# Where the three products of the second transform stand on TensorE in the spectrum of an image tokenizer

## The chip, the cores and the metric

The kernel runs on one core of one Trainium2 chip. The metric is device time in microseconds (us) of one execution; a time given for a kernel is the median of its runs.

## The reference

The reference takes 192 images (64 x 3 channels) of 224 x 224 values, forms the magnitude of their two-dimensional spectrum, crops it to 192 x 192 frequencies, sorts these by radius into 16 rings, projects each ring to a token, and then runs an attention layer, a second attention layer and a mixture of eight experts. Only the first line matters here; everything behind it is the same in both kernels.

```python
f = jnp.fft.fftshift(jnp.fft.fft2(images))
...
power = jnp.abs(f).astype(jnp.float32)
...
power_sorted = power.reshape(B, C, CROP * CROP)[:, :, idx]
```

## The kernel before

The first stage, the function `spectrum`, computes the magnitudes of the 97 x 97 frequencies that the symmetries leave. All data is float32. It works in units of two images (96 units), and two units make a group of four images (48 groups). Each of the five engines has a program of its own, written out by hand: a loop over units or groups, in which a step issues the work of several units at different lags. An engine takes its instructions strictly in this order, and counters (semaphores) tie the engines together. One unit u of group g passes through these places:

- SyncE loads the images of a group into `img`, a ring of four (L203).
- GpSimd adds the two halves of the group's images into `fold` (L255, the even part), and VectorE subtracts them (L367, the odd part). `fold` is a ring of two groups. They count `fold_done` and `odd_fold`.
- TensorE, first transform (`first_dft`, L288): eight products of 97 columns into the PSUM tile `ps1`, a ring of two units. Before the first of a group it waits for `fold_done` and `odd_fold` (L280, L281), and before each unit for `folded_done` at u - 1 (L282): the columns of unit u - 2 must have been folded, since `ps1` is used again. The last one counts `dft1_done`.
- ScalarE copies half of it to SBUF (`far`, L316), after `dft1_done`.
- VectorE folds the columns, one addition and one subtraction (`folded`, L360), and counts `folded_done`.
- TensorE, second transform (`second_dft`): one product of 388 columns (L297) and two of 194 columns (L300) into `ps2`, also a ring of two. It waits for `folded_done` of its unit and for `uv_done` at u - 1, that is, until the unit two before has been combined. The last one counts `dft2_done`.
- ScalarE copies the odd half to SBUF (`odd`, L321), after `dft2_done`; VectorE combines it with the even half (`uv`, L377) and counts `uv_done`; ScalarE squares (L328) and counts `sq_done`; GpSimd sums the squares of a group (`ss`, L262, two instructions); ScalarE takes the root into `power` (L334). SyncE then stores `power` to the table in HBM (L211).

Float32 products run as two passes each, so the trace has 16 first passes in a unit, then 2 of L297 and 4 of L300, and as many weight loads.

The order of each engine's step t is what the change and the prediction turn on:

- TensorE: first transform of unit t, then second transform of unit t - 2.
- ScalarE: `far` of t, `odd` of t - 2, square of t - 4, and in every second step (odd t) a root.
- VectorE: in every second step (even t) the odd part of the next group (L367), then columns of t, then combine of t - 2.
- GpSimd, by groups: even part of group g (L255), then the sum of group g - 3 (L262), which waits for the squares of that whole group.

Weights are loaded for every pass. In the first transform a piece of `fold` (112 columns) is the weight and the table of cosines and sines, `dft`, streams; in the second `dft` is the weight and `folded` streams.

After the stage, all engines wait until the table is stored, and GpSimd gathers the rings from it (L487).

Of the kernel before, what the change touches and what calls it, by code (L numbers as in the profile page):

```python
# [14 lines left out]
BATCH, CHANNELS, SIDE = 64, 3, 224  # L15
IMGS = BATCH * CHANNELS
HALF = SIDE // 2
CROP = 192
FREQ = CROP // 2 + 1
PAIR = 2 * FREQ  # L20
# [102 lines left out]
def at_least(eng, sem, n):  # L123

    if not (isinstance(n, int) and n <= 0):
        eng.wait_ge(sem, n)


def pipeline(eng, step, first, loops, end):


    for t in range(first):
        step(t, t)
    for start, stop, unroll in loops:
        with eng.Fori(start // unroll, stop // unroll) as body:
            for j in range(unroll):
                step(body * unroll + j, start + j)
        first = stop
    for t in range(first, end):
        step(t, t)  # L140
# [4 lines left out]
UNITS = IMGS // 2  # L145
# [5 lines left out]
UPG = G_IMGS // 2  # L151
# [3 lines left out]
Y_RING, FOLD_RING, A_RING, UV_RING, SS_RING = 4, 2, 4, 2, 2  # L155
BODY_G = 4
BODY_U = BODY_G * UPG
S2_LAG = 2
# [3 lines left out]
def spectrum(nc, ctx, sem, xh, table, dft_in, power, w_tok, wt, wt_in, load_constants):  # L162
# [6 lines left out]
    fold = sb("fold", [HALF, FOLD_RING, 2, G_IMGS * SIDE])  # L169
    dft = sb("dft", [HALF, PAIR])  # L170
    far = sb("far", [HALF, 2, 2, PAIR])
    folded = sb("folded", [HALF, A_RING, 2, 2, PAIR])
# [3 lines left out]
    ps1 = ctx.enter_context(nc.psum_tensor("ps1", [P, 2, 2, 512], F32))  # L176
    ps2 = ctx.enter_context(nc.psum_tensor("ps2", [P, 2, 2, 512], F32))
# [5 lines left out]
    dft1_done = sem("dft1_done")  # L183
    far_done = sem("far_done")
    folded_done = sem("folded_done")
    dft2_done = sem("dft2_done")
# [88 lines left out]
    def program_tensor(pe):  # L275
        pe.wait_ge(dft_in_s, 16)

        def first_dft(u, j):
            if j % UPG == 0:
                pe.wait_ge(fold_done, u // UPG + 1)  # L280
                pe.wait_ge(odd_fold, u // UPG + 1)  # L281
            at_least(pe, folded_done, u - 1)  # L282
            for i in range(2):
                for chunk in range(2):
                    for part in range(2):
                        x0 = ((j % UPG) * 2 + i) * SIDE + chunk * HALF
                        col = chunk * PAIR + part * FREQ
                        last = pe.matmul(ps1[0:HALF, j % 2, i, col:col + FREQ],  # L288
                                         fold[:, j // UPG % FOLD_RING, part, x0:x0 + HALF],
                                         dft[:, part * FREQ:(part + 1) * FREQ], start=True, stop=True)  # L290
            last.then_inc(dft1_done, 1)

        def second_dft(u, j):
            pe.wait_ge(folded_done, u + 1)
            at_least(pe, uv_done, u - 1)
            src = folded[:, j % A_RING]
            pe.matmul(ps2[0:FREQ, j % 2, 0, 0:2 * PAIR], dft[:, 0:FREQ], src[:, 0], start=True, stop=True)  # L297
            out = ps2[0:FREQ, j % 2, 1, 0:2 * PAIR].rearrange("p (i c) -> p i c", i=2)
            for part in range(2):
                last = pe.matmul(out[:, :, part * FREQ:(part + 1) * FREQ], dft[:, FREQ:PAIR],  # L300
                                 src[:, 1, :, (1 - part) * FREQ:(2 - part) * FREQ], start=True, stop=True)
            last.then_inc(dft2_done, 1)

        def step(t, j):
            if not isinstance(t, int) or t < UNITS:
                first_dft(t, j)
            if not isinstance(t, int) or t >= S2_LAG:
                second_dft(t - S2_LAG, j - S2_LAG)

        pipeline(pe, step, BODY_U, [(BODY_U, UNITS, BODY_U)], UNITS + S2_LAG)  # L310

    def program_scalar(act):
# [1376 lines left out]
```

## Time and profile before

| | us |
|---|---|
| runs of the kernel before | 925.77, 939.22, 938.95 |
| median | 938.95 |
| span of the profiled execution | 899.4 |
| median less span | 39.6 |
| spectrum stage in the profile, start to the last root | 312.9 |

The profile shows one execution; its own time is not listed, only the span from its first to its last instruction, and what lies around the span (launch and end) is not in the trace. In what follows "PE" is TensorE's stream of matmuls, "PEld" its weight loads, DVE VectorE, ACT ScalarE, POOL GpSimd. A bracket behind a row of the timeline is idle time of that engine just before the row, and what the profile takes for the end of it. The end of a matmul in the trace is modelled, so starts are the safer numbers.

### The profile page before, as it was taken

To read this page: it belongs to the slowest core of one execution; us is meant where nothing else is said; L and a number is where in the kernel's file an instruction comes from. 1 tells how busy PE (TensorE), PEld (TensorE's weight loads), DVE (VectorE), ACT (ScalarE), POOL (GpSimd) and SP (SyncE) were. 2 spreads that over 40 slices of the span, in tenths; PEclk is the share of its full clock that TensorE was granted. 3 is DMA by queue.
4 is the path that set the end of the run, shared out by engine and by line. 5 is a ranking of instruction groups with operands and counts; after the bars stand their busy time and mean duration, and the time that the engine had idled before them with its cause. 6 is when DMAs were issued, how large, how long until landed. Compare 5 with 4: busy or idle time off the path is not lost.

```text
span 899.4 us, 16681 instructions
## 1 busy us (share of the span) xinstructions
PE 737.3 (82%) x5723; PEld 628.5 (70%) x5724; DVE 543.7 (60%) x1003; ACT 429.6 (48%) x821; POOL 425.8 (47%) x363
## 2 busy tenths in 40 slices
PE   5999999999999502889988889968998659999920
PEld 4888888888888402878888886754666637999920
DVE  3899999999999404555555556986667431222224
ACT  1777777777777702444454443313122104555500
POOL 3577777777877407777777770021001161000044
PEclk9999999999999856899999999997669559999975
DMA  8844448854788177554555556000005531111112
GB/s 228 216 123 128 143 124 232 239 152 116 211 224 286 51 208 206 157 150 143 148 158 148 157 147 181 6 2 0 1 1 213 166 107 52 48 52 51 45 56 69
DMA packets 81353, 115.66 MB, mean 129 GB/s; under 512 B 10999, under 2 KB 61148, under 8 KB 80924
## 3 DMA queue, kind: packets, MB, share of 16 engines
q1 hardware_dynamic: 69918, 81.84, 32.0%
q0 software_dynamic: 11392, 33.24, 13.0%
q8 instruction: 28, 0.46, 0.2%
q14 instruction: 15, 0.12, 0.0%
HBM read 91.75 MB, written 23.30 MB: 128 GB/s over the span
## 4 chain that ended last, share of the span: by engine, by line
PE 44%; POOL 20%; DVE 18%; issue 9%; DMA 5%; ACT 2%; DVEq 0%; SPq 0%; POOLq 0%; ACTq 0%
POOL rows L487 15%; PE ps L288 10%; PE psum L1337 6%; DVE folded L360 4%; DVE fold L367 4%; PE ps L300 4%; PE ps L297 4%; PE psum L1324 4%; DVE uv L377 3%; PE psum L898 3%; DMA power_table<-power 3%; PE psum L1327 2%; POOL power L1270 2%; PE psum L919 2%; PE psum L907 2%
## 5 line engine op out<-in xcount | busy, mean ns | idle before, releaser
L546 PE MATMUL psum<-power,tT 128*128 128x192 f32 x864 | 157.9, 340 | 69.0 <-DVE tT L658 68.6
L546 PEld LDWEIGHTS psum<-power,tT 128*128 128x128 f32 x864 | 145.1, 197 | 79.2 <-issue 53.7
L288 PE MATMUL ps<-dft,fold 112*112 112x97 f32 x1536 | 170.9, 266 | 18.9 <-POOL fold L255 10.6
L288 PEld LDWEIGHTS ps<-dft,fold 112*112 112x112 f32 x1536 | 165.2, 181 | 27.6 <-DVE folded L360 15.3
L487 POOL DMA_INDIRECT rows<-power_table,rank_row x144 | 145.1, 1008 | 71.2 <-issue 43.3
L262 POOL TENSOR_TENSOR ss<-uv 97x388 f32<-97x388 f32 x96 | 119.4, 1266 | 77.9 <-ACT uv L328 77.9
L597 ACT ACTIVATE scaled<-rows,swaps 128x384 f32<-128x384 f32 x144 | 80.6, 607 | 127.6 <-DMA rows<-power_table,rank_row 127.5
L658 DVE SCALAR_TENSOR_TENSOR tT<-rows,swaps,scaled 128x384 f32<-128x384 f32 x144 | 82.7, 617 | 82.2 <-ACT scaled L597 80.8
L360 DVE TENSOR_TENSOR folded<-ps,far 112x388 f32<-112x388 f32 x192 | 98.6, 554 | 18.8 <-ACT far L316 18.8
L255 POOL TENSOR_TENSOR fold<-img 112x896 f32<-112x896 f32 x48 | 102.0, 2126 | 13.3 <-DMA img<-in_x 7.1
L377 DVE TENSOR_TENSOR uv<-ps,odd 97x388 f32<-97x388 f32 x192 | 98.6, 555 | 14.3 <-ACT odd L321 12.7
L367 DVE TENSOR_TENSOR fold<-img 112x896 f32<-112x896 f32 x48 | 79.4, 1653 | 9.0 <-DMA img<-in_x 9.0
L300 PEld LDWEIGHTS ps<-folded,dft 112*97 112x97 f32 x384 | 62.7, 163 | 31.5 <-issue 31.0
L328 ACT ACTIVATE uv<-uv 97x776 f32<-97x776 f32 x96 | 81.0, 845 | 0.0
L300 PE MATMUL ps<-folded,dft 112*97 112x194 f32 x384 | 79.1, 327 | 0.0
L297 PE MATMUL ps<-folded,dft 112*97 112x388 f32 x192 | 78.5, 491 | 0.4 <-DVE uv L377 0.4
L334 ACT ACTIVATE power<-ss 97x776 f32 (+1 forms) x48 | 75.7, 1577 | 0.4 <-POOL ss L262 0.4
L1270 POOL DMA_INDIRECT power<-expert_outputs,moe_slot x18 | 17.0, 945 | 123.6 <-DMA expert_outputs<-moe_y 118.5
L321 ACT ACTIVATE odd<-ps 97x388 f32<-97x388 f32 x96 | 47.1, 491 | 52.0 <-PE ps L300 52.0
L730 POOL TENSOR_SCALAR mv<-mv 128x3 f32<-128x3 f32 x6 | 1.5, 252 | 144.6 <-DVE mv L743 144.6
L316 ACT ACTIVATE far<-ps 112x388 f32<-112x388 f32 x96 | 49.0, 511 | 31.2 <-PE ps L288 31.2
L1363 ACT ACTIVATE z<-psum,moe_w_now 128x128 f32<-128x128 f32 x144 | 39.7, 375 | 33.3 <-PE psum L1327 33.1
(158 smaller groups left out, 923.0 us busy)
## 6 DMA issues: line engine op xcount, KB each, us to landing
img<-in_x SPq DMA_DIRECT2D x48, 784.0 KB, 5.2
power_table<-power SPq DMA_DIRECT2D x16, 576.0 KB
power<-in_w_tok SPq DMA_DIRECT2D x3, 1728.0 KB, 10.4
power_table<-power SPq DMA_DIRECT2D x1, 4656.0 KB
power<-in_w SPq DMA_DIRECT2D x8, 579.0 KB, 7.8
power<-in_w SPq DMA_DIRECT2D x4, 1152.0 KB, 10.7
rows<-power_table,rank_row POOLq DMA_INDIRECT x144, 3.1
expert_inputs<-zeros SPq DMA_DIRECT2D x1, 2304.0 KB, 11.0
```

The source lines that it names most:

```text
L255: pool.tensor_tensor(fold[:, j % FOLD_RING, 0], img[:, j % Y_RING, 0], img[:, j % Y_RING, 1], ALU.add).then_inc(fold_done, 1)
L262: last = pool.tensor_tensor(ss[:, j % SS_RING, s], uv[:, j % UV_RING, s, :, 0:FREQ], uv[:, j % UV_RING, 1 - s, :, FREQ:PAIR], ALU.add)
L288: last = pe.matmul(ps1[0:HALF, j % 2, i, col:col + FREQ], fold[:, j // UPG % FOLD_RING, part, x0:x0 + HALF], dft[:, part * FREQ:(part + 1) ...
L297: pe.matmul(ps2[0:FREQ, j % 2, 0, 0:2 * PAIR], dft[:, 0:FREQ], src[:, 0], start=True, stop=True)
L300: last = pe.matmul(out[:, :, part * FREQ:(part + 1) * FREQ], dft[:, FREQ:PAIR], src[:, 1, :, (1 - part) * FREQ:(2 - part) * FREQ], start=T ...
L328: act.activation(v, v, ACT.Square).then_inc(sq_done, 1)
L360: last = dve.tensor_tensor(folded[:, j % A_RING, part], near, far[:, j % 2], op)
L367: dve.tensor_tensor(fold[:, j % FOLD_RING, 1], img[:, j % Y_RING, 0], img[:, j % Y_RING, 1], ALU.subtract).then_inc(odd_fold, 1)
L377: last = dve.tensor_tensor(uv[:, j // UPG % UV_RING, part, i0:i0 + 2, :], even, odd[:, j % 2], op)
L487: pool.indirect_dma_start(out=rows[:, j % RING, half, :], out_offset=None, in_=table[0:RECORDS if j < PLAIN else ROWS, :], in_offset=bass. ...
L546: last = pe.matmul(ps[:, q % 2, 0:DIM], points[:, j % SWAPPED, c, s].rearrange("p h b -> p (h b)"), wt[:, c, s, chunk, :], start=(chunk == ...
L658: last = dve.scalar_tensor_tensor(out=points[:, j % SWAPPED].rearrange("p c s h b -> p (c s) h b")[:, :, half, :], in0=kept, scalar=swaps[ ...
```

## The change

On TensorE alone, a step no longer issues eight products of unit t and then three of unit t - 2. It first waits for all that either part needs, and then issues them mixed: two first products, the second transform's product of 388 columns, two first, one of 194, two first, the other of 194, two first. The products, their operands and their targets are the same, and so are the programs of the other engines. Two counters move with them: `dft2_done` is raised before the last two first products, and `dft1_done` at the very end of the step. The wait for `uv_done` moves from behind the eight first products to the head of the step.

```diff
-        def first_dft(u, j):
+        def first_ready(u, j):
             if j % UPG == 0:
                 pe.wait_ge(fold_done, u // UPG + 1)
                 pe.wait_ge(odd_fold, u // UPG + 1)
             at_least(pe, folded_done, u - 1)
...
-        def second_dft(u, j):
+        def second_ready(u):
             pe.wait_ge(folded_done, u + 1)
             at_least(pe, uv_done, u - 1)
...
         def step(t, j):
-            if not isinstance(t, int) or t < UNITS:
-                first_dft(t, j)
-            if not isinstance(t, int) or t >= S2_LAG:
-                second_dft(t - S2_LAG, j - S2_LAG)
+            dyn = not isinstance(t, int)
+            firsts, seconds = dyn or t < UNITS, dyn or t >= S2_LAG
+            if firsts:
+                first_ready(t, j)
+            if seconds:
+                second_ready(t - S2_LAG)
+            for n, (i, chunk, part) in enumerate((i, c, p) for i in range(2) for c in range(2) for p in range(2)):
+                if firsts:
+                    last = first_dft(j, i, chunk, part)
+                    if n == 7:
+                        last.then_inc(dft1_done, 1)
+                if seconds and n == 1:
+                    second_even(j - S2_LAG)
+                if seconds and n in (3, 5):
+                    last = second_odd(j - S2_LAG, n // 2 - 1)
+                    if n == 5:
+                        last.then_inc(dft2_done, 1)
```

`first_dft` now issues one product of the eight, `second_even` the product of 388 columns and `second_odd` one of the two of 194, with the operands that they had.

On TensorE, two steps in the loop of the stage before the change, an even one and the odd one behind it (`ps1` and `ps2` are the PSUM tiles of the first and the second transform; the names in brackets are the counters waited for):

```order
L126 REGISTER_ALU [waits odd_fold,fold_done]
L288 MATMUL ps1<-dft,fold 112x97 [waits folded_done]
L288 MATMUL ps1<-dft,fold 112x97 x7
L297 MATMUL ps2<-folded,dft 97x388 [waits uv_done,folded_done]
L300 MATMUL ps2<-folded,dft 97x2x97 x2
L288 MATMUL ps1<-dft,fold 112x97 [waits folded_done]
L288 MATMUL ps1<-dft,fold 112x97 x7
L297 MATMUL ps2<-folded,dft 97x388 [waits uv_done,folded_done]
L300 MATMUL ps2<-folded,dft 97x2x97 x2
```

And the even step and the head of the odd one at the same place after it:

```order
L126 REGISTER_ALU [waits odd_fold,fold_done]
L287 MATMUL ps1<-dft,fold 112x97 [waits uv_done,folded_done]
L287 MATMUL ps1<-dft,fold 112x97
L296 MATMUL ps2<-folded,dft 97x388
L287 MATMUL ps1<-dft,fold 112x97 x2
L301 MATMUL ps2<-folded,dft 97x2x97
L287 MATMUL ps1<-dft,fold 112x97 x2
L301 MATMUL ps2<-folded,dft 97x2x97
L287 MATMUL ps1<-dft,fold 112x97 x2
L287 MATMUL ps1<-dft,fold 112x97 [waits uv_done,folded_done]
L287 MATMUL ps1<-dft,fold 112x97
L296 MATMUL ps2<-folded,dft 97x388
```

The wait for `uv_done` has gone from the row of the 388-column product to the row that opens the step, and the step now ends with two products of the first transform, where it ended with two of the second.

The second place is the end of the stage on TensorE, from the last products of the loop's last step to the two steps that have no first transform left. Before:

```order
L288 MATMUL ps<-dft,fold 112x97 x7
L297 MATMUL ps<-folded,dft 97x388 [waits uv_done,folded_done]
L300 MATMUL ps<-folded,dft 97x2x97 x2
L135 REGISTER_ALU
L135 COMPARE_AND_BRANCH
L297 MATMUL ps<-folded,dft 97x388 [waits uv_done,folded_done]
L300 MATMUL ps<-folded,dft 97x2x97 x2
```

And after:

```order
L287 MATMUL ps<-dft,fold 112x97 x2
L301 MATMUL ps<-folded,dft 97x2x97
L287 MATMUL ps<-dft,fold 112x97 x2
L135 REGISTER_ALU
L135 COMPARE_AND_BRANCH
L296 MATMUL ps<-folded,dft 97x388 [waits uv_done,folded_done]
L301 MATMUL ps<-folded,dft 97x2x97 x2
```

The last products of the first transform now stand directly ahead of the next step's second transform, where three longer products stood between. The program of ScalarE, which waits for both counters, is the same row for row: `far` of unit t, then `odd` of unit t - 2, then the square of unit t - 4.

## Rows read from the trace of the kernel before

**Rows 1.** The page: the span of the profiled execution.

```profile
span 899.4 us, 16681 instructions
```

**Rows 2.** Windows of the stage: busy us (instructions) by engine, granted clock, DMA.

```profile
200.00:300.00 100.00, 97.00 (x728) 82.88 (x726) 90.13 (x147) 78.00 (x117) 75.46 (x50) 1.00 0.69 205
```

**Rows 3.** Waits until 310 us: engine, line, releaser, us in total, times, longest.

```profile
POOL ss L262 <- ACT uv L328: 77.9, 48, 6.2
...
PEld ps L300 <- issue: 31.0, 192, 0.2
...
PE ps L288 <- DVE folded L360: 8.3, 22, 0.4
...
PE ps L297 <- DVE uv L377: 0.4, 1, 0.4
```

**Rows 4.** Timeline: start, us, engine, line, tiles; TensorE and the way to its wait.

```profile
144.23 1.81 PE L288 MATMUL ps<-dft,fold 112*112 112x97 f32 x16 [0.41 <-DVE folded L360]
...
147.19 1.72 PE L288 MATMUL ps<-dft,fold 112*112 112x97 f32 x16
...
150.06 1.72 PE L288 MATMUL ps<-dft,fold 112*112 112x97 f32 x16
150.26 0.49 ACT L321 ACTIVATE odd<-ps 97x388 f32<-97x388 f32 x1 [0.82 <-PE ps L300]
...
150.65 0.84 ACT L328 ACTIVATE uv<-uv 97x776 f32<-97x776 f32 x1
...
151.57 2.56 POOL L262 TENSOR_TENSOR ss<-uv 97x388 f32<-97x388 f32 x2 [1.79 <-ACT uv L328]
151.62 0.82 PE L297 MATMUL ps<-folded,dft 112*97 112x388 f32 x2
...
152.27 0.82 PE L300 MATMUL ps<-folded,dft 112*97 112x194 f32 x4
...
152.94 1.72 PE L288 MATMUL ps<-dft,fold 112*112 112x97 f32 x16
...
154.09 2.09 POOL L255 TENSOR_TENSOR fold<-img 112x896 f32<-112x896 f32 x1
...
156.31 1.81 PE L288 MATMUL ps<-dft,fold 112*112 112x97 f32 x16 [0.34 <-DVE folded L360]
...
168.56 0.63 PE L288 MATMUL ps<-dft,fold 112*112 112x97 f32 x4 [0.43 <-DVE folded L360]
```

**Rows 5.** Timeline of the same steps: weight loads, ScalarE and VectorE between them.

```profile
151.74 1.65 DVE L367 TENSOR_TENSOR fold<-img 112x896 f32<-112x896 f32 x1
...
152.77 0.53 ACT L316 ACTIVATE far<-ps 112x388 f32<-112x388 f32 x1
152.77 1.72 PEld L288 LDWEIGHTS ps<-dft,fold 112*112 112x112 f32 x16
...
153.20 0.48 ACT L321 ACTIVATE odd<-ps 97x388 f32<-97x388 f32 x1
153.34 1.03 DVE L360 TENSOR_TENSOR folded<-ps,far 112x388 f32<-112x388 f32 x2
...
154.28 1.02 DVE L377 TENSOR_TENSOR uv<-ps,odd 97x388 f32<-97x388 f32 x2
...
154.69 0.49 ACT L316 ACTIVATE far<-ps 112x388 f32<-112x388 f32 x1 [0.27 <-PE ps L288]
...
155.22 1.03 DVE L360 TENSOR_TENSOR folded<-ps,far 112x388 f32<-112x388 f32 x2
```

**Rows 6.** Timeline at the end of the stage, its last two steps.

```profile
300.58 0.49 ACT L316 ACTIVATE far<-ps 112x388 f32<-112x388 f32 x1 [0.29 <-PE ps L288]
...
301.70 0.81 PE L297 MATMUL ps<-folded,dft 112*97 112x388 f32 x2
...
302.42 1.03 DVE L377 TENSOR_TENSOR uv<-ps,odd 97x388 f32<-97x388 f32 x2 [0.28 <-ACT odd L321]
...
303.60 0.86 PE L297 MATMUL ps<-folded,dft 112*97 112x388 f32 x2 [0.43 <-DVE uv L377]
```

More of the change, by code:

```diff
@@ L282, in first_dft @@
             at_least(pe, folded_done, u - 1)
[L283 to L290, printed above, removed]
@@ L291, in first_dft @@
-            last.then_inc(dft1_done, 1)
-        def second_dft(u, j):
+        def first_dft(j, i, chunk, part):
+            x0 = ((j % UPG) * 2 + i) * SIDE + chunk * HALF
+            col = chunk * PAIR + part * FREQ
+            return pe.matmul(ps1[0:HALF, j % 2, i, col:col + FREQ],
+                             fold[:, j // UPG % FOLD_RING, part, x0:x0 + HALF],
+                             dft[:, part * FREQ:(part + 1) * FREQ], start=True, stop=True)
+        def second_ready(u):
             pe.wait_ge(folded_done, u + 1)
@@ L295, in second_dft, with second_even, second_odd @@
             at_least(pe, uv_done, u - 1)
-            src = folded[:, j % A_RING]
-            pe.matmul(ps2[0:FREQ, j % 2, 0, 0:2 * PAIR], dft[:, 0:FREQ], src[:, 0], start=True, stop=True)
+        def second_even(j):
+            return pe.matmul(ps2[0:FREQ, j % 2, 0, 0:2 * PAIR], dft[:, 0:FREQ], folded[:, j % A_RING, 0],
+                             start=True, stop=True)
+        def second_odd(j, part):
             out = ps2[0:FREQ, j % 2, 1, 0:2 * PAIR].rearrange("p (i c) -> p i c", i=2)
-            for part in range(2):
-                last = pe.matmul(out[:, :, part * FREQ:(part + 1) * FREQ], dft[:, FREQ:PAIR],
-                                 src[:, 1, :, (1 - part) * FREQ:(2 - part) * FREQ], start=True, stop=True)
@@ L302, in second_dft @@
-            last.then_inc(dft2_done, 1)
+            return pe.matmul(out[:, :, part * FREQ:(part + 1) * FREQ], dft[:, FREQ:PAIR],
+                             folded[:, j % A_RING, 1, :, (1 - part) * FREQ:(2 - part) * FREQ], start=True, stop=True)
         def step(t, j):
-            if not isinstance(t, int) or t < UNITS:
-                first_dft(t, j)
-            if not isinstance(t, int) or t >= S2_LAG:
-                second_dft(t - S2_LAG, j - S2_LAG)
+            dyn = not isinstance(t, int)
```

## The prediction

> **What bounds the kernel now.** I read the page first, then the windows of the stage, the waits, and a timeline of some steps, row by row. The span is 899.4 us [rows 1]; the stage that the change touches lies in its first third. In it TensorE is busy 97 us of 100, VectorE 90, ScalarE 78 and GpSimd 75, at full granted clock (1.00, the level of 2.4 GHz) [rows 2]. That looks like a stage bound by TensorE, but 97% of a busy engine isn't yet a bound: it also waits, 22 times, for 8.3 us together [rows 3]. So the timeline has to say what a round of the pipeline costs, and what closes it.
>
> A step of TensorE that starts without a wait takes 2.87 us (147.19 to 150.06), one behind a wait 2.96 (144.23 to 147.19) [rows 4]. Four steps of 2.87 would be 11.48. The rows that wait stand at 144.23, 156.31 and 168.56 [rows 4]: four steps apart, two groups, 12.08 and 12.25 us, mean 12.17. A round of four steps thus has some 0.6 us that isn't TensorE's own work, half a microsecond of waiting and a slower first step.
>
> Who is waited for? The profile names the folding of the columns (L360). The counter in the code says otherwise. The unit that starts at 156.31 is number 48 (counting the 16-pass rows from the start); it asks for `folded_done` 47, that is, units 0 to 46, and the columns of unit 46 end at 153.34 + 1.03 = 154.37 [rows 5]. It also opens a group, and so asks for the even part of that group, which GpSimd makes from 154.09 to 156.18 [rows 4]; 0.13 later TensorE starts. The columns row that ends at 156.25 (155.22 + 1.03) belongs to unit 47, which this step doesn't need [rows 5].
>
> So follow GpSimd back [rows 4]. Its even part (154.09) is queued behind a sum (151.57, 2.56 us); that sum waited for the squares of its group, which is also the longest wait of the whole stage, 77.9 us in 48 times [rows 3]; the square starts at 150.65, the copy `odd` ahead of it at 150.26, and that one waited for TensorE: the end of the step whose successor starts at 150.06. The way from there to 156.31 is 0.20 + 0.39 + 0.92 + 2.52 + 2.22 = 6.25 us. With the two steps before it, 144.23 to 150.06 = 5.83, it makes 12.08: the round. The bound of this stage is a ring of TensorE (two steps), ScalarE (`odd`, square) and GpSimd (sum, even part), and TensorE's throughput lies 5% under it.
>
> **The change part by part.** Nothing is added or removed in work. Three things move, and each touches the ring.
>
> First, `dft1_done` now comes at the end of a step, and ScalarE asks for it (`far` of t) before it looks at `dft2_done` (`odd` of t - 2). Before, `far` was copied while TensorE was still at the second transform, and `odd` started 0.20 us behind the step. Now both counters are late together: `far` follows the last first product. Today `far` starts at 154.69, 0.03 after the end of its 16 passes (152.94 + 1.72) [rows 4, 5]. A pass is 1.56 / 16 = 0.098 us (150.06 to 151.62) and the last of a run ends 0.16 after its successor could start (1.72 - 1.56), so `far` will start about 0.20 after the step's end, where `odd` stands now, and `odd` behind it: 153.20 - 152.77 = 0.43 later [rows 5]. That `dft2_done` itself is raised earlier brings nothing, as `odd` stands behind `far` in ScalarE's queue. Price: 0.43 us in each round. Bounds: 0 (if `far` were copied beside something) and 0.53 (its full duration); I take the row's 0.43. The two others that ask for `dft1_done`, the even and the odd part of the group after next, stay covered: the first products of the step that ends at 150.06 would be through some 0.2 later, and these parts start at 154.09 and 151.74 [rows 4, 5].
>
> Second, the order of the passes. A first pass streams 97 columns; by the 388-column product, 0.65 for two passes (151.62 to 152.27), that is 0.65 / 2 / 4 = 0.081 us of streaming [rows 4], yet it takes 0.098, because a weight load stands before each. Behind a long product the first such load has already been done. Before, a step has one run of first passes behind long ones; after, three, two of which begin inside the step. Each saves at most 0.098 - 0.081 = 0.017, so about 0.03 in a step and 0.06 in the two steps of the ring. Bounds: no gain, and 16 x 0.017 = 0.27 in a step if all loads were hidden. Against the second end stands that weight loads of L300 sat idle for 31.0 us in 192 cases for nothing but their issue [rows 3]: two per unit, 0.16 each, while a long product streamed, so loads aren't drawn further ahead than one.
>
> Third, the wait for `uv_done` stands at the step's head. Before, it came behind eight products and cost 0.4 us once [rows 3]. Now a step t needs the combine of t - 4. Odd steps: `far` at 0.20 behind the step's end, columns 0.53 later (154.69 to 155.22), the combine ends 1.96 after the columns' start (153.34 to 154.28 + 1.02) [rows 5], so 2.69 in all, against 2.84 for the next step's end. Weight loads lead their matmuls by 0.17 (152.77 against 152.94) [rows 4, 5], and from GpSimd's end to TensorE's start it was 0.13; 2.69 + 0.13 + 0.17 - 2.84 = 0.15, so this costs from 0 to 0.15 in an odd step. Even steps: VectorE has the odd part of a group before the columns (151.74 to 153.34 = 1.60), so 2.69 + 1.60 + 1.96 = 6.25 after the end of the odd step; the GpSimd way will take 6.25 + 0.43 = 6.68. Covered by 0.43, while that cover holds. Queued behind the waiting product are the eleven of its own step; who waits for those is `far`, then `odd`. I take 0 for this edit, and 0.15 for its upper end. TensorE would idle near 0.9 us in 12.5 where it idles 0.5 in 12.2; with its clock granted at 1.00 beside that, I count nothing for the clock.
>
> The sum for a round: 0.43 - 0.06 = 0.37 us. One wait to a round, 22 waits [rows 3] are 88 of the 96 steps: 22 x 0.37 = 8.1. The other eight, at the start, save 8 x 0.03 = 0.2. At the end, the last `far` starts at 300.58 and the last second transform, at 303.60, waited for a combine that ends at 302.42 + 1.03 = 303.45, 0.15 before [rows 6]. In the new order that `far` comes 0.20 behind the last step (301.70 + 0.20 = 301.90), its columns at 302.43, the combine behind them ends 1.96 later at 304.39, and TensorE goes on 0.15 after that, at 304.54: 0.9 later. Sum 8.1 - 0.2 + 0.9 = 8.8 us. Everything behind the stage waits for its store, so the span goes from 899.4 to 908.2. The profiled execution's own time isn't given; I put the same 8.8 on the median: 938.95 + 8.8 = 947.8. The three runs spread from 925.77 to 939.22, more than the effect; a change of less than 2% (18.8 us) can hardly be told from none here.
>
> **The rivals.** *VectorE closes the ring after all* (slower). If the profile's naming is right, and TensorE is released by the columns of unit 47, then the way is `odd` at 150.26, combine, odd part, columns, combine, columns [rows 4, 5]. With `far` ahead, VectorE does the columns of unit 45 before that combine, which then ends at 2.69 instead of 151.74 - 150.06 = 1.68 behind the step: 1.01 - 0.06 = 0.95 a round, 22 x 0.95 + 0.7 = 21.6, 960.6 us. It decides once VectorE's way is over 0.43 longer than I have it. For it: VectorE is busy 90 of 100, and the profile's naming; against it: the counter's value, and GpSimd's even part ending 0.13 before the start.
>
> *All loads hidden* (not slower). If loads are drawn under the long products that now stand between the first ones, a step falls by up to 0.27 and a round by 0.54, less 0.43: 22 x -0.11 = -2.4, with -8 x 0.27 = -2.2 at the start and 0.9 at the end -3.7, so 935.2 us. Against it stand the 31.0 us in which loads sat idle beside long products [rows 3]. For it speaks the Trainium skill, page "TensorE: Matmul & The Clock Gate", section "Back-to-back issue gap": matmuls and weight loads are pipelined through a window of 64 instructions; the trace doesn't agree with so deep a look ahead, by those 31.0 us.
>
> *Throughput was the bound* (not slower): the waits are slack elsewhere, and only the 0.03 of a step counts, 96 x 0.03 = 2.9: 936.1. Against it: the 22 waits, each two groups apart.
>
> **How the numbers follow.** Forecast 0.72 (947.8; own range 934.6, which is 925.77 + 8.8, to 953.6, with 0.15 in odd steps and 0.53 for `far`: 22 x 0.25 = 5.5 more, and 0.3, the higher run above the median). VectorE 0.13, loads 0.08, throughput 0.07. The range 934 to 957 holds the forecast, both not-slower cases, and of the VectorE case only what comes when its cover is gone in part. Slower by over 2% is nearly all of that case, 0.12; faster by over 2% needs a low run on top of a gain, 0.02; within 2% is 0.86.
>
> **What would show it.** Right: rounds of 12.5 us; `far` 0.2 behind each step's end, `odd` 0.4 behind `far`; TensorE's idle time before L287 about doubled; the last root ending near 322, against 312.9. Wrong: rounds of 12.1 or less, or of 13 with the combine as what ends the wait.

## The result, and the profile after

The changed kernel takes 944.36 us (median of 22 runs, 931.25 to 955.30) beside 939.09 us (median of 22 runs, 919.38 to 949.31) for the kernel before. Some executions of either kernel, disturbed ones, take some 1.5% longer; the comparison leaves them out, which the two medians don't. By it the ratio is 1.0106, with a 95% interval of 1.0085 to 1.0128, that is 8.0 to 12.0 us of 939, the middle 10.0. The forecast was 8.8 us, and within 2%.

The profile after is one execution of 954.42 us:

```profile
span 952.6 us, 16705 instructions
```

Its span lies 53.2 us above that of [rows 1], which isn't what the change costs. The last root of the stage ends at 320.66 + 1.51 = 322.17 us, where it was 312.87; the stage is 9.3 us longer. The other 43.9 us lie behind it, in code that is the same, where the granted clock differs. Two windows of that part, before and after:

```profile
450.00:550.00 100.00, 88.38 (x539) 81.88 (x538) 55.86 (x87) 46.57 (x87) 67.90 (x69) 1.00 0.51 143
```

```profile
450.00:550.00 100.00, 76.86 (x407) 72.62 (x407) 46.45 (x74) 39.22 (x75) 61.42 (x60) 0.85 0.42 119
```

The third number from the end is the granted clock: 1.00 in that execution of before, 0.85 here, a mean over stretches at either level. In the ten profiles of this study the part behind the stage, the same code in all, took from 587 us (mean clock 0.900 over the span) to 630 us (0.875). So spans can't be compared across these profiles, but the stage can: its clock is 1.00 in all of the loop. I compare by the round, four steps of TensorE, as a mean of 20 rounds from the first pass of step 12 to that of step 92: 46.96 to 290.12 before, 12.158 us; 47.24 to 298.91 after, 12.584. The round is 0.43 us longer; the forecast was 0.37.

The window of the stage, to be read beside [rows 2], busy us (instructions) by engine in the order PE, PEld, DVE, ACT, POOL, then clock and DMA:

```profile
200.00:300.00 100.00, 93.55 (x700) 81.53 (x699) 78.99 (x144) 74.34 (x113) 73.22 (x49) 1.00 0.69 202
```

TensorE's share falls from 97 to 94 with nothing else rising: everyone waits more, so a chain of waits has grown and no engine has. VectorE falls by eleven points, far more than the stage slows; that is told at the end.

The waits until 322 us, beside [rows 3]:

```profile
ACT far L329 <- PE ps L287: 93.0, 74, 12.4
POOL ss L262 <- ACT uv L341: 86.4, 48, 5.2
...
PE ps L287 <- POOL fold L255: 27.9, 23, 11.1
```

TensorE's wait now bears GpSimd's name, which in [rows 3] was VectorE's: 27.9 - 11.1 (the wait for the first image) = 16.8 us in 22 times, where it was 8.3 in 22. And `far` waits for TensorE 74 times, where it was 51, since its counter comes at the step's end.

The timeline of the round that answers to [rows 4]: start, us, engine, line, operation, tiles, and in brackets the idle time before:

```profile
147.94 0.60 PE L287 MATMUL ps<-dft,fold 112*112 112x97 f32 x4 [0.76 <-POOL fold L255]
...
153.31 1.07 PE L287 MATMUL ps<-dft,fold 112*112 112x97 f32 x8
...
153.88 0.49 ACT L329 ACTIVATE far<-ps 112x388 f32<-112x388 f32 x1 [1.23 <-PE ps L287]
...
154.27 0.49 ACT L334 ACTIVATE odd<-ps 97x388 f32<-97x388 f32 x1
...
154.65 0.85 ACT L341 ACTIVATE uv<-uv 97x776 f32<-97x776 f32 x1
...
155.58 2.55 POOL L262 TENSOR_TENSOR ss<-uv 97x388 f32<-97x388 f32 x2 [2.04 <-ACT uv L341]
...
156.29 1.10 DVE L380 TENSOR_TENSOR fold<-img 112x896 f32<-112x896 f32 x1
...
158.09 2.08 POOL L255 TENSOR_TENSOR fold<-img 112x896 f32<-112x896 f32 x1
...
158.34 1.02 DVE L390 TENSOR_TENSOR uv<-ps,odd 97x388 f32<-97x388 f32 x2
...
160.24 1.03 DVE L373 TENSOR_TENSOR folded<-ps,far 112x388 f32<-112x388 f32 x2 [0.88 <-ACT far L329]
...
160.51 0.63 PE L287 MATMUL ps<-dft,fold 112*112 112x97 f32 x4 [0.83 <-POOL fold L255]
```

The row at 153.31 holds the last two products of one step (four passes) and the first two of the next, so the step ends about 4 x 0.098 = 0.39 later, at 153.70. (The row takes 1.07, where eight such passes in a row without a wait take 0.93: the next step, too, starts a little late. That start isn't in the ring.) From there: `far` 0.18 behind, `odd` 0.39 behind `far`, square 0.38, sum 0.93, even part 2.51, next step 2.42: 6.81 us, where [rows 4] had 6.25. The two steps ahead of it take 153.70 - 147.94 = 5.76, where they took 5.83. Three terms can be seen: `far` in front of `odd`, 0.39; the two steps, -0.07; and TensorE starts 160.51 - 160.17 = 0.34 behind the end of the even part, where that was 0.13. Over all groups the median of that distance is 0.24. The last term was in no sum of mine.

The same three terms as means over the 20 rounds, with a step's end taken as the start of its last pass and 0.098 us, or 0.165 where that pass has 194 columns: `odd` starts 0.59 behind the step's end, where it was 0.24, so 0.35; the two steps take 5.75, where they took 5.83, so -0.08; TensorE starts 0.28 behind the even part, where it was 0.13, so 0.15. Together they are 0.42 of the 0.43.

The row at 160.24 also settles whether TensorE asks for the columns that the profile named: they are those of the unit just before, and they end at 161.27, when the step that opens at 160.51 has long been running.

### The profile page after: what moved, and what is told of

The parts are those of the page before. It is cut to its first block, busy times and chain, and to the rows that moved or that the text cites. A ratio compares the mean times of both kernels' runs of the same rounds, so it can differ in the third digit from the quotient of the medians.

```text
span 952.6 us, 16705 instructions
## 1 busy us (share of the span) xinstructions
PE 752.9 (79%) x5723; PEld 649.3 (68%) x5724; DVE 515.3 (54%) x1003; ACT 426.2 (45%) x821; POOL 427.0 (45%) x363
## 4 chain that ended last, share of the span: by engine, by line
PE 52%; issue 16%; POOL 15%; DVE 8%; DMA 3%; another core or an unknown queue 2%; ACT 2%; POOLq 1%; ACTq 0%; DVEq 0%; SPq 0%
PE psum L559 16%; POOL fold L255 8%; PE psum L1350 5%; PE ps L287 5%; POOL ss L262 4%; PE psum L1337 3%; PE psum L911 3%; DMA power_table<-power 2%; PE psum L1340 2%; PE ps L301 2%; PE ps L296 2%; PE psum L542 2%; POOL power L1283 2%; PE psum L932 2%
## 5 line engine op out<-in xcount | busy, mean ns | idle before, releaser
L559 PE MATMUL psum<-power,tT 128*128 128x192 f32 x864 | 171.2, 358 | 91.2 <-DVE tT L671 58.7
L287 PEld LDWEIGHTS ps<-dft,fold 112*112 112x112 f32 x1536 | 197.9, 179 | 63.6 <-issue 47.4
L559 PEld LDWEIGHTS psum<-power,tT 128*128 128x128 f32 x864 | 160.0, 212 | 97.2 <-issue 78.1
L287 PE MATMUL ps<-dft,fold 112*112 112x97 f32 x1536 | 203.6, 262 | 28.7 <-POOL fold L255 27.9
L262 POOL TENSOR_TENSOR ss<-uv 97x388 f32<-97x388 f32 x96 | 119.5, 1267 | 86.4 <-ACT uv L341 86.4
L610 ACT ACTIVATE scaled<-rows,swaps 128x384 f32<-128x384 f32 x144 | 77.8, 604 | 62.9 <-DMA rows<-power_table,rank_row 48.5
L301 PE MATMUL ps<-folded,dft 112*97 112x194 f32 x384 | 94.9, 328 | 0.0
L296 PE MATMUL ps<-folded,dft 112*97 112x388 f32 x192 | 78.6, 491 | 1.3 <-DVE uv L390 1.3
L380 DVE TENSOR_TENSOR fold<-img 112x896 f32<-112x896 f32 x48 | 54.4, 1134 | 9.9 <-DMA img<-in_x 9.9
L1350 PE MATMUL psum<-power,z 128*128 x288 | 53.0, 335 | 0.0
L301 PEld LDWEIGHTS ps<-folded,dft 112*97 112x97 f32 x384 | 48.7, 166 | 0.7 <-issue 0.6
```

The source lines that it names most:

```text
L262: last = pool.tensor_tensor(ss[:, j % SS_RING, s], uv[:, j % UV_RING, s, :, 0:FREQ], uv[:, j % UV_RING, 1 - s, :, FREQ:PAIR], ALU.add)
L287: return pe.matmul(ps1[0:HALF, j % 2, i, col:col + FREQ], fold[:, j // UPG % FOLD_RING, part, x0:x0 + HALF], dft[:, part * FREQ:(part + 1) ...
L296: return pe.matmul(ps2[0:FREQ, j % 2, 0, 0:2 * PAIR], dft[:, 0:FREQ], folded[:, j % A_RING, 0], start=True, stop=True)
L301: return pe.matmul(out[:, :, part * FREQ:(part + 1) * FREQ], dft[:, FREQ:PAIR], folded[:, j % A_RING, 1, :, (1 - part) * FREQ:(2 - part) * ...
L559: last = pe.matmul(ps[:, q % 2, 0:DIM], points[:, j % SWAPPED, c, s].rearrange("p h b -> p (h b)"), wt[:, c, s, chunk, :], start=(chunk == ...
L1350: last = pe.matmul(psum[:, 6 + j % 2, 0:DIM], hT[:, j % 2, m * P:(m + 1) * P], w2[:, bass.ds(e, 1), m, :].rearrange("p a n -> p (a n)"), s ...
```

## The experiments

Each kernel changes one thing and is read by the round. In brackets behind a round stand the starts of steps 12 and 92, 20 rounds apart. The counters are those of the code: `dft1_done` after the first transform, `dft2_done` after the second, `uv_done` after the combine.

**The copy `far` out of the ring's way.** Edit on the changed kernel:

```diff
-                if seconds and n in (3, 5):
-                    last = second_odd(j - S2_LAG, n // 2 - 1)
-                    if n == 5:
+                if seconds and n in (3, 7):
+                    last = second_odd(j - S2_LAG, n // 4)
+                    if n == 7:
```

> The changed kernel, but the second product of 194 columns stands behind all eight first products, so that dft1_done comes before the step's end and dft2_done at it, as in the kernel before; the interleaving and the waits at the step's head stay. A round is four steps of TensorE, the mean from unit 12 to unit 92: 12.16 us before, 12.58 after. Theory (the copy far, queued ahead of odd on ScalarE, lengthens the ring by 0.39): far is copied 0.1 to 0.2 earlier than the step's end, odd starts 0.2 to 0.3 behind it, and the round falls to 12.2 to 12.3. Rival (mixing itself, weight changes or PSUM traffic, costs): the round stays at 12.5 to 12.6. Rival (the waits at the head alone): it stays at 12.5 or more.

Measured: round 12.274 us (47.17 to 292.65). The timeline:

```profile
145.40 0.60 PE L287 MATMUL ps<-dft,fold 112*112 112x97 f32 x4 [0.67 <-POOL fold L255]
...
151.02 0.49 ACT L329 ACTIVATE far<-ps 112x388 f32<-112x388 f32 x1 [1.23 <-PE ps L287]
151.16 0.54 PE L287 MATMUL ps<-dft,fold 112*112 112x97 f32 x4
...
151.41 0.49 ACT L334 ACTIVATE odd<-ps 97x388 f32<-97x388 f32 x1
...
157.64 0.53 PE L287 MATMUL ps<-dft,fold 112*112 112x97 f32 x3 [0.63 <-POOL fold L255]
```

`far` starts 0.14 before the next step (151.16) instead of 0.18 behind, and `odd` 0.25 behind it instead of 0.57. That takes 0.31 of the 0.43 away with the products still mixed. So 0.31 of the loss hangs on which counter is raised last, and none of that on the mixing.

**No mixing, but the same counter last.** Edit on the changed kernel, in the place of its loop over n:

```diff
+            if seconds:
+                second_even(j - S2_LAG)
+                second_odd(j - S2_LAG, 0)
+                second_odd(j - S2_LAG, 1).then_inc(dft2_done, 1)
+            if firsts:
+                for i, chunk, part in ((i, c, p) for i in range(2) for c in range(2) for p in range(2)):
+                    last = first_dft(j, i, chunk, part)
+                last.then_inc(dft1_done, 1)
```

> No mixing at all: the three products of the second transform stand ahead of the eight of the first, with the same waits at the step's head as in the changed kernel. dft1_done comes at the step's end, dft2_done 1.6 us before. Theory (far ahead of odd): the round is 12.5 to 12.7, like the changed kernel's, though nothing is mixed; odd starts 0.39 behind far and far 0.2 behind the step's end. Rival (mixing costs): the round is 12.2 or less.

Measured: round 12.631 us (48.69 to 301.30). The second transform now opens a step (L296 rows):

```profile
149.75 0.86 PE L296 MATMUL ps<-folded,dft 112*97 112x388 f32 x2 [0.72 <-POOL fold L255]
...
152.67 0.82 PE L296 MATMUL ps<-folded,dft 112*97 112x388 f32 x2
...
155.61 0.86 PE L296 MATMUL ps<-folded,dft 112*97 112x388 f32 x2
155.74 0.49 ACT L326 ACTIVATE far<-ps 112x388 f32<-112x388 f32 x1 [1.26 <-PE ps L287]
156.13 0.49 ACT L331 ACTIVATE odd<-ps 97x388 f32<-97x388 f32 x1
...
162.37 0.89 PE L296 MATMUL ps<-folded,dft 112*97 112x388 f32 x2 [0.81 <-POOL fold L255]
```

The row at 155.74 is `far`, right behind the step's end; `odd` follows 0.39 later, though its own products stand at the head of the step that began at 152.67. The loss is all there without any mixing, and 0.05 more, since the mixing's small gain is gone. The rival that mixing itself costs falls with these two runs.

**The wait at the step's head.** Edit on the changed kernel:

```diff
             if seconds:
-                second_ready(t - S2_LAG)
...
                 if seconds and n == 1:
+                    at_least(pe, uv_done, t - S2_LAG - 1)
                     second_even(j - S2_LAG)
```

The two steps without a first transform keep their wait for `folded_done`.

> The changed kernel with the wait for uv_done taken from the step's head to the product of 388 columns, where it stood before, and the doubled wait for folded_done (it asks for the same count) left out; the order of products stays. If the row of waits at the head costs what it seems to (TensorE starts 0.24 to 0.37 behind GpSimd's even part, where it was 0.13), that gap falls to about 0.13 and the round by 0.1 to 0.2, to 12.4 to 12.5, and the second group of a round no longer waits for the combine. If the head's waits cost nothing, the round stays at 12.58.

Measured: round 12.440 us (47.40 to 296.21), 0.14 less. The rows behind a sum:

```profile
157.09 2.08 POOL L255 TENSOR_TENSOR fold<-img 112x896 f32<-112x896 f32 x1
...
159.31 0.63 PE L287 MATMUL ps<-dft,fold 112*112 112x97 f32 x4 [0.63 <-POOL fold L255]
```

TensorE starts 159.31 - 159.17 = 0.14 behind the even part, close to the 0.13 before the change. So more waits queued behind the one that ends last delay the start, though they had long been met: the combine of the step at 160.51 in the changed kernel ended at 158.34 + 1.02 = 159.36, 1.15 before. Which of the two waits taken out does it isn't told apart.

**Both edits together.** The two diffs above at once.

> Both single edits at once on the changed kernel: the second product of 194 columns behind all eight first ones, and the wait for uv_done at the product of 388 columns. Alone they took the round from 12.58 us to 12.27 and to 12.44. If they are two separate terms of one ring, their gains add: 12.58 - 0.31 - 0.14 = 12.13, under the 12.16 of the kernel before by about what the mixing saves TensorE; GpSimd's even part is again 0.13 ahead of the step. If they are one and the same delay seen twice, the round stays near 12.27.

Measured: round 12.135 us (46.65 to 289.35), where 12.13 was expected, so the terms add: 0.31 + 0.14 = 0.45. That is 0.02 under the kernel before, with the products mixed. The rows behind a sum:

```profile
151.79 1.09 DVE L377 TENSOR_TENSOR fold<-img 112x896 f32<-112x896 f32 x1
...
153.58 2.09 POOL L255 TENSOR_TENSOR fold<-img 112x896 f32<-112x896 f32 x1
...
155.81 0.63 PE L287 MATMUL ps<-dft,fold 112*112 112x97 f32 x4 [0.41 <-POOL fold L255]
```

TensorE starts 155.81 - 155.67 = 0.14 behind the even part again. VectorE's odd part takes 1.09 us here, where it took 1.65 before the change [rows 5], and yet the round is within 0.02 of the one before: the length of that part doesn't set it.

**Squares first.** On the changed kernel, ScalarE's step in another order:

```diff
-            if dyn or t < UNITS:
-                far_copy(t, j)
-            if dyn or ODD <= t < UNITS + ODD:
-                odd_copy(t - ODD, j - ODD)
             if dyn or SQ <= t < UNITS + SQ:
                 square(t - SQ, j - SQ)
             if (j - RT) % UPG == 0 and (dyn or t >= RT):
                 root((t - RT) // UPG, (j - RT) // UPG)
+            if dyn or t < UNITS:
+                far_copy(t, j)
+            if dyn or ODD <= t < UNITS + ODD:
+                odd_copy(t - ODD, j - ODD)
```

> The changed kernel, with ScalarE's step in another order: square of t - 4 and root first, then far, then odd. The squares' input is ready before the step starts. If the ring through odd, square, sum and even part bounds the stage, it is cut here, TensorE no longer waits for GpSimd, and what is next is VectorE: combine must end before the step's head, 6.4 us behind the end of the odd step, so the round falls to about 12.1. If VectorE closes the ring already, the round stays at 12.5 or more.

Measured: round 11.603 us (46.34 to 278.40). The direction is that of the theory, the size isn't: 12.1 was expected, from an odd part of 1.60 us in VectorE's way, and it takes 1.10 on average here. With that, the way is 2.69 + 1.1 + 1.96 + 0.13 = 5.88 for two steps, near the 5.80 measured. VectorE does bound this kernel: in the rounds, each step of TensorE starts 0.10 to 0.18 behind the end of the combine that it asks for.

**Squares first in the kernel before.** The same edit on ScalarE, with TensorE's old order.

> The kernel before, with only ScalarE's step in another order: square of t - 4 and root, then far, then odd. TensorE's order is that of before. Theory (ring through odd, square, sum, even part): the round falls from 12.16 us to what TensorE needs for four steps, 11.5, the stage ends 22 x 0.66 = 14 us earlier, so the time falls by 1.5%. Rival (VectorE closed the ring before the change, as the profile named the columns): far and odd come no earlier to VectorE than before, so the round stays at 12.1 to 12.2 and the time within 0.2%.

Measured: round 11.490 us (45.80 to 275.60), time 908.17 us (median of 6 runs) beside 925.42 for the kernel before on the same chip (11 runs), ratio 0.9824, interval 0.9774 to 0.9874. The last root ends at 297.33, where it was 312.87. The window, the waits until 297 us, two groups of instructions (busy us, mean ns), and steps of the timeline:

```profile
100.00:200.00 100.00, 100.00 (x770) 88.51 (x769) 85.01 (x158) 80.73 (x122) 64.47 (x52) 1.00 0.69 185
```

```profile
POOL ss L262 <- ACT uv L328: 99.2, 48, 4.0
...
PE ps L288 <- POOL fold L255: 11.5, 1, 11.5
...
PE ps L297 <- DVE uv L377: 1.0, 1, 1.0
```

```profile
L262 POOL TENSOR_TENSOR ss<-uv 97x388 f32<-97x388 f32 x96 | 82.2, 878 | 99.2 <-ACT uv L328 99.2
...
L367 DVE TENSOR_TENSOR fold<-img 112x896 f32<-112x896 f32 x48 | 54.1, 1126 | 10.2 <-DMA img<-in_x 10.2
```

```profile
140.59 1.72 PE L288 MATMUL ps<-dft,fold 112*112 112x97 f32 x16
140.79 0.49 ACT L321 ACTIVATE odd<-ps 97x388 f32<-97x388 f32 x1 [0.82 <-PE ps L300]
...
141.18 0.84 ACT L328 ACTIVATE uv<-uv 97x776 f32<-97x776 f32 x1
...
142.10 1.71 POOL L262 TENSOR_TENSOR ss<-uv 97x388 f32<-97x388 f32 x2 [1.97 <-ACT uv L328]
...
143.46 1.72 PE L288 MATMUL ps<-dft,fold 112*112 112x97 f32 x16
143.77 2.09 POOL L255 TENSOR_TENSOR fold<-img 112x896 f32<-112x896 f32 x1
...
146.33 1.72 PE L288 MATMUL ps<-dft,fold 112*112 112x97 f32 x16
...
149.21 1.03 PE L288 MATMUL ps<-dft,fold 112*112 112x97 f32 x9
```

Every step is 2.87 us, TensorE is busy 100 us of 100, and its two waits left are the one for the first image and one of 1.0 us for a combine, at 289.57, behind the loop.

What the edit does can be read in the rows. A square still stands behind an `odd` in ScalarE's queue (141.18 behind 140.79), but it is now the square of the next step: each comes one step of TensorE, 2.87 us, earlier. The way from a step's end through `odd`, square, sum and even part is as it was, with a shorter sum: 140.59 to 145.86, and 0.13 more to a start, 5.40 us. But the step that asks for this even part is the third one on, at 149.21, 8.62 us behind 140.59. So the ring isn't cut; it spans three steps in place of two, and has 3.2 us to spare.

On VectorE nothing was edited, and its combine and odd part ask for the same counters; but its odd part got shorter here too (mean 1126 ns, where it was 1653), so this run alone doesn't refute the rival that VectorE closed the ring. With three other readings it does: in the code the step doesn't ask for the columns that the profile named; in the changed kernel it starts before they end (160.24, above); and with both edits together the odd part is as short as here while the round is that of before. So before the change TensorE waited for GpSimd.

**Mixing with TensorE as the bound.** Squares first, mixed products, and the wait for `uv_done` moved back, by the diffs above.

> The changed order of products, squares first on ScalarE, and the wait for uv_done at the product of 388 columns. With the ring cut, only TensorE's own work is left, and the mixing shows alone: two more runs of first passes that begin behind a long product save 0.03 a step, so the round is 11.4, 0.1 under that of the unmixed kernel with squares first; about 2 us less in all. If mixing costs TensorE something that the ring hid, the round is above 11.5.

Measured: round 11.390 us (46.86 to 274.66), with TensorE again at 100 of 100:

```profile
100.00:200.00 100.00, 100.00 (x776) 88.92 (x775) 85.82 (x159) 79.13 (x124) 65.17 (x53) 1.00 0.69 186
```

So the mixing is worth 0.10 us a round, 0.025 a step, as soon as TensorE is the bound: the gain of 0.03 that the prediction gave it is real. In the whole time it doesn't show: 909.44 us, ratio 0.9827 (0.9777 to 0.9878), against 0.9824 without mixing.

**Squares first with the wait left at the head**, timed.

> The changed kernel with squares first, the wait for uv_done still at the step's head; timed beside the two others. Its round was 11.60 in one look, with 0.10 to 0.16 between the end of the combine and the step's head: now VectorE's combine decides when a step may start. Expected: 11.6 again, 12 us under the kernel before, 1 to 2 us above the variant with the wait moved back.

Measured: round 11.603 us again (48.31 to 280.37), time 918.55 us, ratio 0.9853 (0.9796 to 0.9911), that is 13.6 us of 925 where 12 were expected. The round is 0.21 above the variant with the wait moved back; over 22 rounds that is 4.7 us, more than the 1 to 2 expected. In the whole time the three intervals overlap.

## Why the prediction was right

- *The bound* was read rightly: a ring of two steps of TensorE, `odd`, square, sum and even part, not TensorE's 97%, and not the columns that the profile put beside TensorE's wait. The count in the code against the end of the row decided that. The runs bear it out: with one more step of TensorE in the ring no step of the loop waits, and in the changed kernel the step starts before those columns end.
- *First term, `far` ahead of `odd`*: 0.43 predicted, 0.39 in the row of the timeline, 0.35 as a mean over the rounds; moving one product so that `far` comes before the step's end gave 0.31 back.
- *Second term, order of the passes*: 0.06 for two steps predicted; 0.07 in the round shown, 0.08 as a mean, and 0.05 by the two kernels in which TensorE is the bound.
- *Third term, the wait for `uv_done`*: taken as 0, with 0.15 as its end. It cost 0.14, but by another way. The step named was that the combine may come late for an odd step. The combine wasn't late in the steps that close the round; the start was, behind a longer row of waits. That 0.14 lies inside the 0.15 is luck, and so in part is how near 0.37 comes to 0.43: this term, left at nothing, was made up for in part by the first, taken 0.08 too large. Over 22 rounds, 0.14 is 3.1 us.
- *The sum*: 8.1 for the loop, -0.2 for the start and 0.9 for the end, 8.8. Measured in the profiles: between steps 8 and 95 the loop got 8.8 us longer (34.73 to 298.83 before, 34.63 to 307.54 after), the start 0.1 shorter, the end 0.6 longer (312.87 - 298.83 = 14.04, 322.17 - 307.54 = 14.63): 9.3. The whole time's 10.0, with 8.0 to 12.0 as its interval, fits either figure and couldn't have told the terms apart.
- *What VectorE's way takes* was wrong, on the safe side: 6.25 us was given for an even step. The combine at 158.34 ends 159.36 - 153.70 = 5.66 after the step's end. The step that failed is the odd part's 1.60 us, which holds a wait; it took 1.10 here. In the forecast it only served to cover the third term in even steps, and a shorter way covers that better.
- *Around the span*: the 39.6 us between the span and the median weren't launch and end. 954.42 - 952.6 = 1.8 is; the profiled execution of before was a shorter one than the listed runs. Nothing in the sum hung on it, nor on the "some 0.6 us" of a round that isn't TensorE's own work, which is 12.17 - 11.48 = 0.69.
- *Loads hidden* and *throughput* both asked for rounds of 12.2 or less in the changed kernel; neither came. Nor did loads hide where nothing else bounds: mixing is worth 0.025 a step there, not 0.27. *VectorE closes the ring* asked for 0.95 more a round, and it was 0.43.

## What to carry to other kernels

When work of one engine is reordered, what counts is not when each result is ready, but which counter the next engine asks for first: a result raised early behind a counter raised late is worth nothing in a queue that is taken in order. Read a busy share of 97% with its waits, and follow the wait by the counts in the code, since the profile names whoever ended last and not whoever was asked for. And before moving products about, look along the ring for an instruction whose input is ready earlier: putting the squares first on ScalarE gave 1.8% with one block of lines moved.

## What the runs showed of the hardware

VectorE's odd part (L367, L380) and GpSimd's sum (L262) get in each other's way. In [rows 5] the odd part starts at 151.74, 0.17 after the sum in [rows 4], and takes 1.65 us; in the changed kernel it starts at 156.29, 0.71 after the sum, and takes 1.10. With nothing of GpSimd's beside it, it takes 1.08, as in this row of the changed kernel:

```profile
24.68 1.08 DVE L380 TENSOR_TENSOR fold<-img 112x896 f32<-112x896 f32 x1
```

The sum is two instructions. Where no odd part runs beside it, both take 0.87 to 0.88 (mean 878 ns in the kernel before with squares first); beside an odd part the second takes 1.73, and the pair 2.55 as in the timelines. So the odd part first waits out the GpSimd instruction that is under way: its end lies 0.94 behind that of the sum's first instruction in both kernels (0.17 + 1.65 and 0.71 + 1.10, less 0.88). Then the sum's second instruction waits for the odd part: the pair ends 0.74 behind it in both (154.13 - 153.39, 158.13 - 157.39). The Trainium skill, page "SBUF — State Buffer", section "Who interferes with whom", has VectorE's two-tensor operations with both inputs in SBUF contend with GpSimd's reads, and calls the ports that the two share an exclusive lock; the trace agrees, with these numbers.

That collision explains most of the eleven points that VectorE's share fell (its 48 odd parts took 79.4 us before and 54.4 after), why its way was shorter than predicted, and that 0.85 us of the ring before and after (1.73 - 0.88) were such a wait. A version that keeps the two apart and leaves the ring as it is wasn't tried.

Waits that are already met aren't free on TensorE: its start lay 0.13 behind the last releaser with the old row of waits at the head, and at a median of 0.24 with the wait for `uv_done` and a second one for `folded_done` behind it. Taking these two out again gave 0.14 us a round.
